# Reordering VectorE's period, one bank for the gate projection and the tail's last product in a convolution, state-space and expert kernel

## The chip, the cores and the metric

One core of one Trainium2 chip. The metric is the device time of one execution in microseconds; lower is better. The kernel before took 418.74 us, the median of 3 runs (417.58 to 419.7).

## The reference, cut to what matters

Three layers run over x of shape (16, 64, 16, 16) in float32: a graph convolution with group norm, a selective state-space layer on 64 features of 256 tokens for each of the 16 images, and a top-2-of-8 expert layer. The change touches the last two.

```python
# state-space layer, per token t (INNER = 128 channels, 16 states)
x_main, x_gate = split(ln(x) @ W_in + b_in)
xc = silu(x_main @ W_conv + b_conv)
B, C = split(xc @ W_bc + b_bc);  dt = softplus(xc @ W_dt + b_dt)
h = exp(dt * A) * h + dt * B * xc        # the scan over tokens
y = sum over states of (h * C)
t = t + (y * silu(x_gate)) @ W_out + b_out
# expert layer
xn = ln(ln(t));  logits = ln(t) @ Wr + br;  top 2 of 8, softmax weights
t = t + sum over the 2 chosen experts of w * (gelu(xe @ W1 + b1) @ W2 + b2)
```

## The kernel before, in words

The 16 images go in G = 8 groups of two; a group has T = 512 token columns on 128 partitions. The 2,048 state rows of a group (128 channels by 16 states) are 16 blocks of 128 rows, taken two at a time in 8 **slots**. A slot on VectorE is a product that forms the scan's input (L736, in the first group's slots 0 and 1 L731) and the scan itself (L743). GpSimd then multiplies the scan's result by C (`pool_slot`, L341), and TensorE sums over the states (`pe_sum`, L1023). The decay factors exp(dt * A) come from ScalarE (`act_decay`, L572), blocks 0 to 7 from a copy that DMA spreads over the partitions, blocks 8 to 15 from TensorE (`pe_spread`, L1098).

The loop over i has 8 **periods**, here called period 0 to period 7. In period i the slots of group i run; beside them goes the rest of group i - 1 (`prev`: gate product, output projection, norm, router, experts) and the beginning of group i + 2 (`nxt2`: first norm, projections). Nothing is planned by a program: each engine has its own hand-written order in its own `body`, and semaphores tie them together.

On VectorE a period is slot 0, `dve_relu` (L758, the softplus' linear part for group i + 1), `dve_gate` (L764, y times the silu of the gate), `dve_t1` (L768, projection plus residual, which waits for TensorE's `pe_po`, L1077), slot 1, then `dve_lnF` (L774), `dve_xn2` (L781 twice and L785 twice, the operand X2 of the first expert matrix, its high part), `dve_router1` (L790, L793, L796), `dve_xn` of group i + 2 (L749), `dve_router2` (ten small instructions, L803 to L822), slots 2 to 7 with the eight `dve_expert` (L830) from slot 4 on. `dve_router2` needs an exponential from ScalarE (`act_router`, L592), which ScalarE gives after `act_lnA2` (L517, L519) of group i + 2. GpSimd makes the low part of X2 by a subtraction (`pool_x2`, L366), and ends the router's weights (`pool_router`, L372 to L383). ScalarE's second half of a period is the experts' gelu (L610), then `act_siluz` (L526) and `act_silug` (L531) of group i + 2.

PSUM has 8 banks of 512 columns: 0 and 1 hold the scan's input, 2 B, then XD, XA, XB, XC = 3 to 6, and YS = 7. `pe_projg` (L1052) writes the gate projection into XC, which the experts' sums use too, and so waits for `me`, VectorE's reading of experts 4 and 5. `pe_warm` (L1174) issues matmuls whose result nobody reads.

After the last period the rest of group 7 runs with nothing beside it; this is called the **tail** here: gate, output projection, norm, router and experts. In period 7 the last product by C is GpSimd's like all others.

Of the kernel before, what the change touches and what calls it, by code (L numbers as in the profile page):

```python
# [70 lines left out]
def build(nc, x, cW1, cb1, Wl, bl, Wr, Wf, bf, cW2, cb2, W_in, b_in, W_conv, b_conv, A_log, W_bc, b_bc,  # L71
# [10 lines left out]
    with ctx:  # L82
# [140 lines left out]
        gp = nc.gpsimd  # L223

# [161 lines left out]
        def _(eng):  # L386
# [71 lines left out]
            def body(i, p, nxt, nxt2, prev):  # L458
# [36 lines left out]
                pool_slot(eng, i, p, 7)  # L495
# [7 lines left out]
            pool_x2(eng, G - 1)  # L503
# [24 lines left out]
        def act_silug(eng, g):  # L528
            eng.wait_ge(S["g_mm"], g + 1)
            since(eng, "yg", g - 2)  # L530
            a_.activation(sg[:, g % 3, :], P[:, XC, :], ACT.Silu, bias=cols[:, R["b_in"] + 1:R["b_in"] + 2]).then_inc(S["sg"], 1)  # L531
# [46 lines left out]

        def act_lnF2(eng, g):
            eng.wait_ge(S["var2"], g + 1)  # L580
            since(eng, "tn", g)
            a_.activation(rs2[:, :], P[:, XB, HW:T], ACT.Ln, bias=epst[:, 0:1]).then_inc(S["ln2"], 1)
            since(eng, "xn2", 2 * g)
            a_.activation(rqs[:, :], P[:, XB, HW:T], ACT.Ln, scale=1.0 + EPS, bias=eps2t[:, 0:1]).then_inc(S["lnq"], 1)
            eng.wait_ge(S["ln2"], g + 1)
            a_.activation(rs2[:, :], rs2[:, :], ACT.Exp, scale=-0.5).then_inc(S["rs2"], 1)
            eng.wait_ge(S["lnq"], g + 1)
            a_.activation(rqs[:, :], rqs[:, :], ACT.Exp, scale=-0.5).then_inc(S["rq"], 1)
# [24 lines left out]
        def _(eng):  # L613
# [22 lines left out]
            def body(i, p, nxt, nxt2, prev):  # L636

                q = 1 - p
                act_decay(eng, i, 4, 5, 6, 7)
# [13 lines left out]
                act_decay(eng, i, 12, 13)  # L653
                if nxt2 is not None:
                    act_lnA2(eng, nxt2)
                if prev is not None:
                    act_router(eng, prev)
# [45 lines left out]
            a_.preload_act_table_set("natural_log_exp_and_others")  # L703
            act_abs(eng, 1)
# [71 lines left out]
        def dve_xn2(eng, g):  # L776
            eng.wait_ge(S["rq"], g + 1)
            since(eng, "xl2", g)
            for h in range(2):
                q = slice(64 * h, 64 * h + 64)  # L780
                v.tensor_tensor(xnt2[:, HW * h:HW * h + HW], P[q, XB, 0:HW], rqs[q, :], ALU.mult).then_inc(S["xn2"], 1)  # L781
            since(eng, "f1", EXP * KC * g)
# [52 lines left out]
        def _(eng):  # L835
# [122 lines left out]
            def body(i, p, nxt, nxt2, prev):  # L958
# [11 lines left out]
                elif nxt is not None:  # L970
                    dve_relu(eng, nxt)
                if prev is not None:
                    dve_gate(eng, prev)
                    dve_t1(eng, prev, q)
                dve_slot(eng, i, 1)
                if i == 0:
                    dve_relu(eng, 1)
                if prev is not None:
                    dve_lnF(eng, prev)
                    dve_xn2(eng, prev)  # L980
                    dve_router1(eng, prev)
                if i > 0 and nxt2 is not None:
                    dve_xn(eng, nxt2)
                if prev is not None:
                    dve_router2(eng, prev)
                dve_slot(eng, i, 2)
                if i == 0:
# [418 lines left out]
```

## Time and profile before

| | us |
|---|---|
| median of 3 runs | 418.74 |
| the profiled execution | 418.46 |
| its span, first to last instruction | 416.7 |
| VectorE busy | 335.4 (80% of the span) |
| TensorE busy (ends are modelled) | 339.8 (82%) |
| ScalarE busy | 279.7 (67%) |
| GpSimd busy | 269.7 (65%) |

The profiled execution is 0.28 us below the median of the runs, and its span 1.8 us below its own time. Times of the trace count from the start of the span. A group of the page or a line of the timeline names the source line, engine, instruction, what it writes and reads, and in brackets how long the engine sat idle before it and what ended that wait.

### The profile page before, as it was taken

The numbers are of one execution on the slowest core, as the hardware profiler recorded it, in microseconds if no ns is written. First come the engines' busy times: TensorE is split into PE (matmuls) and PEld (weight loads), VectorE is DVE, ScalarE is ACT, GpSimd is POOL, SyncE is SP. The second block draws the span as 40 slices with busy tenths as digits, with TensorE's granted clock in tenths as the row PEclk, the third lists the DMA queues.
The fourth block names the chain that finished last, engine by engine and source line by source line (L and its number), as shares of the span: only waits on it lengthen the run. The fifth ranks groups of instructions, "written<-read, shape, count | busy, mean of one in ns | idle before, by whom it ended". The sixth has DMA issues, their size and how long they took to land. (4 is left out here: it accounts for less than half of the span.)

```text
span 416.7 us, 5478 instructions
## 1 busy us (share of the span) xinstructions
PE 339.8 (82%) x1651; PEld 181.9 (44%) x1651; DVE 335.4 (80%) x460; ACT 279.7 (67%) x458; POOL 269.7 (65%) x272
## 2 busy tenths in 40 slices
PE   0596896728898889888988999799789977996795
PEld 0483444412454345434543553455245524543452
DVE  2786456697899989998999899899989999992411
ACT  1002667736976996799779879987896767650563
POOL 9615125575559947995799489848975894683222
PEclk9996998668999999999999899999988998996999
DMA  8680089899769478769865887579767960000000
GB/s 198 194 155 4 0 208 226 218 230 226 186 160 212 115 192 194 170 138 196 206 165 132 201 201 170 142 170 223 167 150 167 223 145 0 2 0 14 1 0 13
DMA packets 21236, 59.52 MB, mean 143 GB/s; under 512 B 4924, under 2 KB 13272, under 8 KB 15320
## 3 DMA queue, kind: packets, MB, share of 16 engines
q1 hardware_dynamic: 20040, 58.34, 61.1%
q10 hardware_dynamic: 1168, 0.84, 0.8%
q8 instruction: 13, 0.21, 0.2%
q14 instruction: 15, 0.12, 0.1%
HBM read 53.93 MB, written 5.24 MB: 142 GB/s over the span
## 5 line engine op out<-in xcount | busy, mean ns | idle before, releaser
L341 POOL TENSOR_TENSOR hs<-hs,Cs 128x1024 f32<-128x1024 f32 x64 | 151.8, 2372 | 53.7 <-DVE hs L743 53.1
L743 DVE TENSOR_TENSOR_SCAN hs<-av,P 128x1024 f32<-128x1024 f32 x64 | 146.3, 2286 | 4.9 <-PE P L1023 2.0
L610 ACT ACTIVATE hb<-P,b1c 128x512 f32<-128x512 f32 x128 | 81.4, 683 | 21.5 <-PE P L1145 19.2
L736 DVE SCALAR_TENSOR_TENSOR P<-P,bbcol,ub 128x1024 f32<-128x1024 f32 x62 | 79.7, 1285 | 1.3
L1158 PE MATMUL P<-hb,W2s 128*64 128x256 f32 x512 | 68.7, 391 | 0.0
L1144 PE MATMUL P<-X,W1H 128*128 128x512 f32 x128 | 59.6, 465 | 5.2 <-ACT hb L610 3.3
L1145 PE MATMUL P<-X,W1L 128*128 128x512 f32 x128 | 52.2, 408 | 0.0
L353 POOL TENSOR_TENSOR accs<-accs,mes 128x256 f32<-128x256 f32 x56 | 40.9, 731 | 12.0 <-DVE mes L830 7.4
L572 ACT ACTIVATE av<-P,Aneg 128x510 f32<-128x510 f32 x68 | 44.0, 687 | 6.7 <-PE P L1098 5.4
L1158 PEld LDWEIGHTS P<-hb,W2s 128*64 128x64 f32 x512 | 31.3, 136 | 30.6 <-issue 20.5
L830 DVE SCALAR_TENSOR_TENSOR mes<-P,cols,wbs 128x256 f32<-128x256 f32 x64 | 27.3, 467 | 16.0 <-PE P L1158 9.6
L572 ACT ACTIVATE av<-av,Aneg 128x510 f32<-128x510 f32 x60 | 38.1, 707 | 0.1
L1144 PEld LDWEIGHTS P<-X,W1H 128*128 128x128 f32 x128 | 25.1, 196 | 26.9 <-ACT hb L610 15.9
L1098 PE MATMUL P<-D,selD 128*128 128x512 f32 x64 | 32.6, 535 | 4.9 <-ACT av L572 4.0
L1023 PE MATMUL P<-hs,selS 128*32 128x512 f32 x256 | 31.8, 623 | 5.3 <-POOL hs L341 5.3
L603 ACT ACTIVATE wbs<-P 128x512 f32<-128x512 f32 x32 | 19.1, 598 | 20.8 <-PE P L1132 20.8
L1145 PEld LDWEIGHTS P<-X,W1L 128*128 128x128 f32 x128 | 25.3, 198 | 2.8
L1174 PE MATMUL P<-W1H 128*128 128x512 f32 x62 | 21.9, 475 | 4.6 <-POOL X L366 4.6
L1098 PEld LDWEIGHTS P<-D,selD 128*128 128x128 f32 x64 | 11.8, 194 | 18.9 <-issue 18.3
L1023 PEld LDWEIGHTS P<-hs,selS 128*32 128x32 f32 x256 | 6.9, 112 | 28.6 <-issue 16.9
L366 POOL TENSOR_TENSOR X<-xnt,X 64x512 fp32r<-64x512 f32 x8 | 10.1, 1264 | 12.4 <-DVE X L785 10.9
L1062 PE MATMUL P<-xc,Wrep 128*128 128x512 f32 x16 | 9.8, 696 | 9.1 <-DVE P L736 9.1
(188 smaller groups left out, 489.7 us busy)
## 6 DMA issues: line engine op xcount, KB each, us to landing
ub<-u_scratch SPq DMA_DIRECT2D x31, 1024.0 KB, 10.7
av<-dt_scratch SPq DMA_DIRECT2D x15, 1024.0 KB, 7.2
dt_scratch<-dts SPq DMA_DIRECT2D x7, 256.0 KB, 2.8
u_scratch<-rl SPq DMA_DIRECT2D x7, 256.0 KB, 2.8
av<-in_L_conv_Wr SPq DMA_DIRECT2D x2, 576.0 KB, 7.2
av<-in_L_conv_Wl SPq DMA_DIRECT2D x2, 576.0 KB, 7.7
res<-in_x SPq DMA_DIRECT2D x4, 256.0 KB, 4.8
hb<-in_L_ffn_W SPq DMA_DIRECT2D x2, 512.0 KB, 6.1
```

Source lines behind the costliest of these rows:

```text
L341: gp.tensor_tensor(hs[:, at, :, :], hs[:, at, :, :], rep(Cs[:, p, :], 1, 2), ALU.mult).then_inc(S["cm"], 1)
L353: gp.tensor_tensor(acc[:, p, :], prev, mes[:, e % 4, :], ALU.add).then_inc(S["acc"], 1)
L572: a_.activation(steps, dt_of, ACT.Exp, scale=Aneg[:, m:m + 1]).then_inc(S["aexp"], 1)
L610: a_.activation(hb[:, r % 4, :], P[:, (XA, XB)[r % 2], :], ACT.Gelu, bias=b1c[:, r:r + 1]).then_inc(S["gl"], 1)
L736: v.scalar_tensor_tensor(out=ring, in0=rep(P[:, BB, :], 1, 2), scalar=bbcol[:, 0:1], in1=ub[:, 2 * n:2 * n + 2, :], op0=ALU.add, op1=ALU.m ...
L743: v.tensor_tensor_scan(hs[:, (SLOTS * g + n) % RING].rearrange("p a t -> p (a t)"), av[:, 2 * n:2 * n + 2, :].rearrange("p a t -> p (a t)" ...
L830: v.scalar_tensor_tensor(out=mes[:, e % 4, :], in0=P[:, (XC, XD)[e // 2 % 2], HW * (e % 2):HW * (e % 2) + HW], scalar=cols[:, R["b2"] + e: ...
L1023: last = pe.matmul(P[32 * q:32 * q + 32, YS, :], selS[:, k, :], hs[:, (SLOTS * g + n) % RING, q % 2, :], start=(k == 0), stop=(k == 3))
L1098: pe.matmul(P[:, (YS, XA)[m % 2], :], selD[:, m - BY_PE[0], :], D2[:, :], start=True, stop=True).then_inc(S["dt_pe"], 1)
L1144: pe.matmul(P[:, bank, :], W1H[:, e, 128 * k:128 * k + 128], X2[:, :], start=True, stop=False)
L1145: pe.matmul(P[:, bank, :], W1L[:, e, 128 * k:128 * k + 128], X2[:, :], start=False, stop=True).then_inc(S["f1"], 1)
L1158: last = pe.matmul(P[64 * h:64 * h + 64, (XC, XD)[pair % 2], HW * (e % 2):HW * (e % 2) + HW], W2s[:, e, k, :], hb[:, r % 4, HW * h:HW * h ...
```

## The change

In words: the gate projection of groups 2 to 7 goes to bank XB and waits for the previous gelus instead of `me`. VectorE runs the gate product ahead of the relu, and both router parts ahead of `dve_xn`; ScalarE gives the router's exponential ahead of `act_lnA2`. In the first period two decays (blocks 4 and 5) go ahead of ScalarE's softplus of group 1, the relu of group 1 behind slot 2, and the norm product of group 2 from behind slot 3 to behind slot 5. In a normal period 2 instead of 4 warming matmuls stand before the experts. In the last period VectorE does the last product by C itself, and 10 warming matmuls stand before the last sum over states. In the tail ScalarE makes the experts' scale before the router's, VectorE does the experts' operand around the router's and its low part, and 3 instead of 8 warming matmuls follow the router.

```diff
+        def gbank(g):
+            return XC if g < 2 else XB
...
   # GpSimd
                 weighted(4)
-                pool_slot(eng, i, p, 7)
+                if nxt is not None:
+                    pool_slot(eng, i, p, 7)
...
-            pool_x2(eng, G - 1)
             pool_router(eng, G - 1)
...
   # ScalarE: act_silug reads P[:, gbank(g), :] instead of P[:, XC, :]
...
         def act_lnF2(eng, g):
             eng.wait_ge(S["var2"], g + 1)
             since(eng, "tn", g)
             since(eng, "xn2", 2 * g)
+            since(eng, "xh2", 2 * g)
+            if g < G - 1:
+                act_rs2(eng, g)
+                act_rq(eng, g)
+                act_rs2_exp(eng, g)
+                act_rq_exp(eng, g)
+            else:
+                act_rq(eng, g)
+                act_rs2(eng, g)
+                act_rq_exp(eng, g)
+                act_rs2_exp(eng, g)
...
-                act_decay(eng, i, 4, 5, 6, 7)
+                act_decay(eng, i, *((4, 5, 6, 7) if i > 0 else (6, 7)))
...
                 act_decay(eng, i, 12, 13)
+                if prev is not None:
+                    act_router(eng, prev)
                 if nxt2 is not None:
                     act_lnA2(eng, nxt2)
-                if prev is not None:
-                    act_router(eng, prev)
...
             a_.preload_act_table_set("natural_log_exp_and_others")
+            act_decay(eng, 0, 4, 5)
             act_abs(eng, 1)
             act_softplus(eng, 1)
...
   # VectorE: dve_xn2 gets an argument, called between its two xnt2 products and its two X2 products
...
                 dve_slot(eng, i, 0)
                 if i == 0:
                     dve_xn(eng, 1)
-                elif nxt is not None:
+                if prev is not None:
+                    dve_gate(eng, prev)
+                if i > 0 and nxt is not None:
                     dve_relu(eng, nxt)
                 if prev is not None:
-                    dve_gate(eng, prev)
                     dve_t1(eng, prev, q)
                 dve_slot(eng, i, 1)
-                if i == 0:
-                    dve_relu(eng, 1)
                 if prev is not None:
                     dve_lnF(eng, prev)
                     dve_xn2(eng, prev)
                     dve_router1(eng, prev)
+                    dve_router2(eng, prev)
                 if i > 0 and nxt2 is not None:
                     dve_xn(eng, nxt2)
-                if prev is not None:
-                    dve_router2(eng, prev)
                 dve_slot(eng, i, 2)
+                if i == 0:
+                    dve_relu(eng, 1)
...
                 dve_slot(eng, i, 3)
-                if i == 0:
-                    dve_xn(eng, 2)
                 dve_slot(eng, i, 4)
                 experts(0)
                 dve_slot(eng, i, 5)
+                if i == 0:
+                    dve_xn(eng, 2)
                 experts(2)
...
                 dve_slot(eng, i, 7)
+                if nxt is None:
+                    last = hs[:, (SLOTS * G - 1) % RING, :, :]
+                    eng.wait_ge(S["cm"], SLOTS * G - 1)
+                    eng.wait_ge(S["scan"], SLOTS * G)
+                    v.tensor_tensor(last, last, rep(Cs[:, p, :], 1, 2), ALU.mult).then_inc(S["cm"], 1)
                 experts(6)
...
             dve_t1(eng, G - 1, 1)
-            dve_lnF(eng, G - 1)
+            dve_xn2(eng, G - 1, lambda: dve_lnF(eng, G - 1))
+            eng.wait_ge(S["xh2"], 2 * G)
+            v.tensor_tensor(X2[64:128, :], xnt2[:, :], X2[0:64, :], ALU.subtract).then_inc(S["xl2"], 1)
             dve_router1(eng, G - 1)
-            dve_xn2(eng, G - 1)
             dve_router2(eng, G - 1)
...
   # TensorE
         def pe_projg(eng, g):
-            since(eng, "cs", g)
-            if g == 1:
-                eng.wait_ge(S["sg"], 1)
-            since(eng, "me", EXP * (g - 2) - 2)
+            if g < 2:
+                since(eng, "cs", g)
+                since(eng, "sg", g)
+            since(eng, "gl", EXP * KC * (g - 2))
...
-                    pe_warm(eng, 4, XB)
+                    pe_warm(eng, 2, XB)
...
                 for k in range(4):
+                    if k == 3 and nxt is None:
+                        pe_warm(eng, 10, XB)
                     pe_sum(eng, i, k)
...
             pe_router(eng, G - 1)
-            pe_warm(eng, 8)
+            pe_warm(eng, 3)
```

## Rows read from the trace of the kernel before

**Rows 1.** Windows view: most of period 3; two microseconds of period 4.
```profile
core 0: us, PE busy (x) PEld busy (x) DVE busy (x) ACT busy (x) POOL busy (x), PEclk, DMA share, GB/s
181.00:221.00 40.00, 35.60 (x182) 18.21 (x182) 37.53 (x48) 33.70 (x57) 30.97 (x28) 1.00 0.78 176
232.00:234.00 2.00, 2.00 (x6) 1.15 (x4) 1.93 (x6) 1.36 (x2) 1.07 (x5) 0.50 1.09 233
```

**Rows 2.** Timeline of VectorE, period 4: start us, us, instruction, idle before.
```profile
222.56 0.48 DVE L768 SCALAR_TENSOR_TENSOR t1s<-P,cols,res 128x256 f32<-128x256 f32 x1 [0.76 <-PE P L1077]
...
230.18 0.42 DVE L749 TENSOR_TENSOR xnt<-P,rs 128x256 f32<-128x256 f32 x1 [0.90 <-ACT rs L519]
...
232.40 1.28 DVE L736 SCALAR_TENSOR_TENSOR P<-P,bbcol,ub 128x1024 f32<-128x1024 f32 x1
```

**Rows 3.** Timeline of VectorE, period 7, which has no relu and no first norm.
```profile
340.50 0.69 DVE L764 TENSOR_TENSOR ygs<-P,sg 128x512 f32<-128x512 f32 x1 [0.18 <-PE P L1023]
341.95 0.48 DVE L768 SCALAR_TENSOR_TENSOR t1s<-P,cols,res 128x256 f32<-128x256 f32 x1 [0.76 <-PE P L1077]
...
348.96 0.97 DVE L803 SCALAR_TENSOR_TENSOR rt<-rt,rank 128x32 f32<-128x32 f32 x1 [0.30 <-ACT rt L592]
...
351.64 1.28 DVE L736 SCALAR_TENSOR_TENSOR P<-P,bbcol,ub 128x1024 f32<-128x1024 f32 x1
```

**Rows 4.** Timeline of GpSimd, its subtraction for X2 in periods 4 and 7.
```profile
229.23 1.26 POOL L366 TENSOR_TENSOR X<-xnt,X 64x512 fp32r<-64x512 f32 x1 [0.23 <-POOL hs L341]
...
348.62 1.26 POOL L366 TENSOR_TENSOR X<-xnt,X 64x512 fp32r<-64x512 f32 x1 [0.23 <-POOL hs L341]
```

**Rows 5.** Timeline of TensorE, the gate projection in period 3.
```profile
212.90 1.10 PE L1052 MATMUL P<-xnt,Wgs 128*128 128x256 f32 x4 [1.24 <-DVE mes L830]
```

**Rows 6.** Timeline of VectorE, period 0 and the first scan of period 1.
```profile
61.45 1.23 DVE L731 TENSOR_TENSOR P<-P,hs 128x1024 f32<-128x1024 f32 x1 [1.76 <-PE P L1109]
...
67.59 0.75 DVE L758 TENSOR_SCALAR rl<-P,cols 128x512 f32<-128x512 f32 x1 [2.58 <-ACT sp L536]
...
70.28 2.29 DVE L743 TENSOR_TENSOR_SCAN hs<-av,P 128x1024 f32<-128x1024 f32 x1 [0.74 <-DVE P L736]
...
79.82 0.42 DVE L749 TENSOR_TENSOR xnt<-P,rs 128x256 f32<-128x256 f32 x1 [3.60 <-ACT rs L519]
...
91.16 1.29 DVE L736 SCALAR_TENSOR_TENSOR P<-P,bbcol,ub 128x1024 f32<-128x1024 f32 x1
...
98.17 2.29 DVE L743 TENSOR_TENSOR_SCAN hs<-av,P 128x1024 f32<-128x1024 f32 x1 [1.97 <-PE P L1023]
```

**Rows 7.** Timeline of ScalarE, period 0: softplus of group 1, decays 8 and 9.
```profile
66.87 0.69 ACT L536 ACTIVATE sp<-P,cols 128x512 f32<-128x512 f32 x1
...
72.34 1.26 ACT L572 ACTIVATE av<-P,Aneg 128x510 f32<-128x510 f32 x2 [0.92 <-POOL rl L328]
```

**Rows 8.** Page, DMA issues: KB each, median us from issue to landing.
```profile
ub<-u_scratch SPq DMA_DIRECT2D x31, 1024.0 KB, 10.7
```

**Rows 9.** Timeline of VectorE, the last scan and the tail.
```profile
373.19 2.29 DVE L743 TENSOR_TENSOR_SCAN hs<-av,P 128x1024 f32<-128x1024 f32 x1
...
379.95 0.69 DVE L764 TENSOR_TENSOR ygs<-P,sg 128x512 f32<-128x512 f32 x1 [3.71 <-PE P L1023]
...
387.84 0.20 DVE L790 TENSOR_TENSOR P<-P,brs 128x32 f32<-128x32 f32 x1 [0.71 <-PE P L1115]
...
390.66 0.96 DVE L807 TENSOR_TENSOR rt<-rt,rv 128x32 f32<-128x32 f32 x1
```

**Rows 10.** Timeline of GpSimd, its subtraction for X2 in the tail.
```profile
390.31 1.26 POOL L366 TENSOR_TENSOR X<-xnt,X 64x512 fp32r<-64x512 f32 x1 [10.86 <-DVE X L785]
```

**Rows 11.** Timeline of TensorE, the last sum over states.
```profile
377.95 1.94 PE L1023 MATMUL P<-hs,selS 128*32 128x512 f32 x8 [3.58 <-POOL hs L341]
```

**Rows 12.** Timeline of ScalarE, first logarithm of the second norm, period 7 and tail.
```profile
344.70 0.47 ACT L582 ACTIVATE rs2s<-P,epst 128x256 f32<-128x256 f32 x1 [0.21 <-PE P L1087]
...
385.53 0.47 ACT L582 ACTIVATE rs2s<-P,epst 128x256 f32<-128x256 f32 x1 [1.28 <-PE P L1087]
```

More of the change, by code:

```diff
@@ L530, in act_silug @@
             since(eng, "yg", g - 2)
-            a_.activation(sg[:, g % 3, :], P[:, XC, :], ACT.Silu, bias=cols[:, R["b_in"] + 1:R["b_in"] + 2]).then_inc(S["sg"], 1)
+            a_.activation(sg[:, g % 3, :], P[:, gbank(g), :], ACT.Silu, bias=cols[:, R["b_in"] + 1:R["b_in"] + 2]).then_inc(S["sg"], 1)
         def act_abs(eng, g):
@@ L577, in act_lnF1, with act_rs2, act_rq, act_rs2_exp @@
             a_.activation(sq2[:, :], P[:, XB, 0:HW], ACT.Square).then_inc(S["sq2"], 1)
+        def act_rs2(eng, g):
+            a_.activation(rs2[:, :], P[:, XB, HW:T], ACT.Ln, bias=epst[:, 0:1]).then_inc(S["ln2"], 1)
+        def act_rq(eng, g):
+            a_.activation(rqs[:, :], P[:, XB, HW:T], ACT.Ln, scale=1.0 + EPS, bias=eps2t[:, 0:1]).then_inc(S["lnq"], 1)
+        def act_rs2_exp(eng, g):
+            eng.wait_ge(S["ln2"], g + 1)
+            a_.activation(rs2[:, :], rs2[:, :], ACT.Exp, scale=-0.5).then_inc(S["rs2"], 1)
+        def act_rq_exp(eng, g):
+            eng.wait_ge(S["lnq"], g + 1)
+            a_.activation(rqs[:, :], rqs[:, :], ACT.Exp, scale=-0.5).then_inc(S["rq"], 1)
         def act_lnF2(eng, g):
@@ L581, in act_lnF2 @@
             since(eng, "tn", g)
-            a_.activation(rs2[:, :], P[:, XB, HW:T], ACT.Ln, bias=epst[:, 0:1]).then_inc(S["ln2"], 1)
             since(eng, "xn2", 2 * g)
[L584 to L588, printed above, removed]
+            since(eng, "xh2", 2 * g)
[9 more added lines that the diff above has]
+                act_rs2_exp(eng, g)
         def act_router(eng, g):
@@ L774, in dve_lnF, with dve_xn2 @@
             v.tensor_tensor(tns[:, :], P[:, XB, 0:HW], rs2[:, :], ALU.mult).then_inc(S["tn"], 1)
-        def dve_xn2(eng, g):
+        def dve_xn2(eng, g, between=None):
             eng.wait_ge(S["rq"], g + 1)
@@ L781, in dve_xn2 @@
                 v.tensor_tensor(xnt2[:, HW * h:HW * h + HW], P[q, XB, 0:HW], rqs[q, :], ALU.mult).then_inc(S["xn2"], 1)
+            if between is not None:
+                between()
             since(eng, "f1", EXP * KC * g)
@@ L1046, in pe_projg @@
         def pe_projg(eng, g):
-            since(eng, "cs", g)
-            if g == 1:
-                eng.wait_ge(S["sg"], 1)
-            since(eng, "me", EXP * (g - 2) - 2)
+            if g < 2:
+                since(eng, "cs", g)
+                since(eng, "sg", g)
+            since(eng, "gl", EXP * KC * (g - 2))
             for h in range(2):
-                last = pe.matmul(P[:, XC, HW * h:HW * h + HW], Wgs[:, h, :], xnt[:, :], start=True, stop=True)
+                last = pe.matmul(P[:, gbank(g), HW * h:HW * h + HW], Wgs[:, h, :], xnt[:, :], start=True, stop=True)
             last.then_inc(S["g_mm"], 1)
```

## The prediction

> **What bounds the kernel now.** I read the windows first, then the timeline of VectorE, then the waits that interrupt it, and only then the other engines. Over 40 us that are most of period 3, VectorE is busy 37.53 of 40.00 us, TensorE 35.60 at full clock, ScalarE 33.70 and GpSimd 30.97 [rows 1]. VectorE runs its slots back to back and has two stops in a normal period: 0.76 us ahead of t1, while TensorE forms the output projection, and 0.90 us ahead of the first norm's product, while ScalarE ends its scale [rows 2]. So VectorE sets the length of the six periods 1 to 6, and an edit there is worth what it takes from these stops. At both ends of the kernel VectorE is not full: in period 0 it stands 2.58, 0.74 and 3.60 us [rows 6], and in the tail one engine waits for another all along. There each link of the chain counts.
>
> **Gate ahead of relu (periods 1 to 6).** Period 7 has no relu and shows the new order: the gate product starts after 0.18 us of waiting for the sum over states, and t1 follows 1.45 us after the gate (341.95 - 340.50) [rows 3]. The relu (0.75 [rows 6]) now fits between them, since 0.69 + 0.75 = 1.44. The stop of 0.76 goes, 0.18 comes: 0.58 at most. Some of it is lost because an instruction that waits can't start under the end of the one before (an estimate, 0.08 at each of the two places). I take 0.4, with 0.2 and 0.58 as bounds: 6 x 0.4 = 2.4 us. The relu's reader on GpSimd is still busy with an older product by C then, and is not made late.
>
> **Router ahead of the first norm (periods 1 to 5).** Meant to remove the 0.90. But period 7 again shows the new order: 0.30 us of waiting for ScalarE's exponential, and then an L803 of 0.97 us, where it computes only 32 columns [rows 3]; L790, as small, takes 0.20 [rows 9]. Its end, 348.96 + 0.97 = 349.93, lies at the end of GpSimd's subtraction for X2, 348.62 + 1.26 = 349.88 [rows 4]. In the tail L803 comes ahead of that subtraction, and it is L807 that takes 0.96 and ends at 391.62, with the subtraction ending at 391.57 [rows 9, 10]. Both instructions read two tensors from SBUF, as the subtraction does. So I read 0.78 us as a hold by GpSimd. In period 4 the subtraction ends at 230.49, just ahead of where L803 comes behind the norm product, which starts at 230.18 [rows 2, 4]: the wait of 0.90 hid the hold. From the end of L796 to slot 2 it takes 0.90 + (232.40 - 230.18) = 3.12 us now; in the new order 0.30 + (351.64 - 348.96) = 2.98 [rows 2, 3], plus 0.42 for the norm product, whose scale is long there: 3.40. That is a loss of 0.28 a period, 5 x 0.28 = 1.4 us. Without the hold it would be 3.40 - 0.78 = 2.62, a gain of 0.5 a period. I take the hold, because two such lengths end together with the same neighbour.
>
> The Trainium skill (SBUF - State Buffer, section "Who interferes with whom") says that a VectorE instruction with two SBUF inputs and a GpSimd instruction that reads SBUF exclude each other, the later one waiting for the whole of the first. By it every one of periods 1 to 5 pays the hold (408.7 in all); were the long instructions something else, the sum would be 404.8.
>
> **Gate projection in XB.** TensorE's wait of 1.24 for `me` goes [rows 5], and ScalarE's silu and table load come that much earlier. VectorE has no wait on ScalarE's decays in a period, so this is off the path: 0, with VectorE's slot 7 as the cover. The two warming matmuls less also cost or give nothing there, as ScalarE's gelu table is the later one. All of it gives slack, and if the cover went it would be worth at most 1.2 a period.
>
> **Period 0.** Slot 1's scan ends at 67.59 - 2.58 = 65.0. Now: the relu waits, slot 2's scan starts at 70.28 because decay 5 is late, slot 4 waits 3.60 for the norm, and slot 7's input product ends at 91.16 + 1.29 = 92.45 [rows 6]. After: decays 4 and 5 take ScalarE's place at 66.87 and end at 66.87 + 1.26 = 68.13 (the price of two from decays 8 and 9) [rows 7]. Slot 2's input product needs only its load (a chunk lands 10.7 us after its issue [rows 8], in the median) and is done by then. Scan 68.2 to 70.5; relu to 71.25. GpSimd's step for group 1, which started when softplus was ready 2.2 us earlier, starts there, and decays 8 and 9, which wait for it at 72.34, start at 74.5 and end at 75.8 [rows 7]. VectorE meanwhile: input product, scan, input product (0.15 + 1.29 + 2.29 + 1.29) to 76.3, so it barely waits. Scan to 78.6, product to 79.9, scan to 82.2. The norm's scale, ready at 79.8, comes at 82.0, no wait. Norm 0.4, then product, scan, product: 87.4. That is 92.45 - 87.4 = 5.0 us. The first scan of period 1 comes 98.17 - 92.45 = 5.72 us after that point, behind TensorE's work that starts there [rows 6], and moves with it. What could be late next: the load of u's first chunk for group 1, behind a write that is issued 2.2 us later (needed by 90 to 92, expected at 89), and GpSimd's restart behind slot 7's product, which I work out at 92.3 against a scan at 93.1. Bounds 2.0 (one of them late) and 5.9 (TensorE at full clock in that stretch).
>
> **Tail.** (a) The last scan ends at 373.19 + 2.29 = 375.48; GpSimd's last product is behind its accumulations, and the sum starts at 377.95 and takes 1.94 at half clock after TensorE sat idle 3.58 [rows 9, 11]. VectorE's product costs 1.23 (the nearest row is L731 of the same shape, with one input in PSUM [rows 6]), so the sum can start at 376.8; ten warming matmuls keep TensorE busy until then, and at full clock it takes half, 1.0. The gate, now at 379.95, comes at 377.9: 2.0 us. The experts' instructions behind the product (0.85) end before. (b) From the gate to the norm's first logarithm it is 385.53 - 379.95 = 5.58 in the tail, and 344.70 - 340.50 = 4.20 in period 7 [rows 3, 9, 12]; the difference is TensorE's half clock. I take 1.3; bounds 0 and 1.4. (c) After it: the wait of 0.71 for the router's product goes under the experts' operand, the hold of 0.96 - 0.20 = 0.76 goes with GpSimd's subtraction [rows 9]; VectorE's subtraction adds 0.62 (half of 1.23) ahead of the router, and the exponential is waited for, 0.30 [rows 3]. 0.71 + 0.76 - 0.62 - 0.30 = 0.55, taken as 0.5; bounds -0.3 and 1.2. After that TensorE runs on as before. The tail gives 3.8.
>
> **Sum.** 2.4 - 1.4 + 5.0 + 2.0 + 1.3 + 0.5 = 9.8 us. The profiled execution took 418.46, so 408.7; it lies 0.28 below the median, which is less than I can resolve, and I predict 408.7.
>
> **Rivals.** No hold in the router: all as above, but the router gains 0.5 a period instead of losing 0.28, 3.9 us more, 404.8. Against it are two coincidences of ends within 0.1 us; for it, that five of these periods showed no long instruction. Period 0 is worth only 2.0 because a load or GpSimd's restart is late: 411.7. For it, everything there is chained; against, each has some slack. The tail's clock does not hold, so the change doesn't do what it says there: the sum costs 1.94 again and (b) gives nothing, 2.2 less, 410.9. Slower: with two warming matmuls instead of four TensorE's clock stays at half through the experts. It fell there even with four, to 0.50 at 232 to 234 [rows 1]. TensorE has 4.40 us idle in a period, and a us at half clock adds 0.5 of work, so from 9 us of half clock a period on it would become the bound. At 13 us in each of 7 periods it costs 6.5 - 4.4 = 2.1 each, 14.7, and gives 418.46 - 9.8 + 14.7 = 423.4. Against it, the row at 0.50 has TensorE fully busy, which is what brought the clock back each time.
>
> **Numbers.** The forecast has 0.62, no hold 0.08, a short period 0 0.17, the tail's clock 0.08, the clock in the periods 0.03; 0.02 is left for a change within the noise. The range 405.0 to 412.0 holds the first, third and fourth with their bounds. About 0.5%, 2.1 us, is what a measurement of this kernel can tell from no change; faster means under 416.6. Faster 0.95, same 0.02, slower 0.03.
>
> **What would show it.** In a normal period: gate first with a wait near 0.2, no wait ahead of t1, an L803 near 0.97 in periods 1 to 7 and no wait ahead of the norm product; a period of 39.8 us instead of 40. Slot 7's input product of period 0 ending at 87.4. The gate of the tail 2.5 us after the last scan instead of 4.5, its sum at about 1.0 us, and no long router instruction. An L803 of 0.18 in periods 1 to 5, a new wait ahead of slots 4 to 6 of period 0 or of slot 0 of period 1, or a TensorE clock of 0.5 over most of the experts would make the prediction wrong.

## The result, and the profile after

The changed kernel takes 408.27 us in the median of 4 runs (406.66 to 409.93), beside 419.06 us (417.58 to 419.7, 4 runs) for the kernel before (its 418.74 further up came from the first three of these runs): a ratio of 0.9751, with a 95% interval of 0.9715 to 0.9787. The forecast was 408.7, in a range of 405.0 to 412.0. The profiled execution of the changed kernel is the slowest of its four, 409.93 us with a span of 408.2; before, the span was 416.7. So the spans differ by 8.5 us, where the forecast's sum was 9.8, and the first question is which terms make 8.5.

I cut both spans at the same points: the start of slot 0's scan in each period, and the start of the last scan. From VectorE's timelines these are 57.09, 98.17, 138.34, 178.32, 218.28, 258.24, 298.22, 338.03 and 373.19 before, and 56.70, 92.61, 132.23, 171.99, 211.73, 251.50, 291.26, 330.69 and 367.17 after.

| stretch | before | after | gained | forecast |
|---|---|---|---|---|
| to the first scan | 57.09 | 56.70 | 0.39 | 0 |
| period 0 | 41.08 | 35.91 | 5.17 | 5.0 |
| periods 1 to 6 | 239.86 | 238.08 | 1.78 | 1.0 |
| period 7 to its last scan | 35.16 | 36.48 | -1.32 | 0 |
| last scan to the end | 43.51 | 41.03 | 2.48 | 3.8 |
| span | 416.7 | 408.2 | 8.5 | 9.8 |

Two lines are off by more than 1 us, period 7 and the tail. First the middle, VectorE's timeline after, in period 2 (start us, us, instruction, idle before it):

```profile
134.68 0.69 DVE L788 TENSOR_TENSOR ygs<-P,sg 128x512 f32<-128x512 f32 x1 [0.17 <-PE P L1055]
135.28 0.74 DVE L782 TENSOR_SCALAR rl<-P,cols 128x512 f32<-128x512 f32 x1
136.12 0.48 DVE L792 SCALAR_TENSOR_TENSOR t1s<-P,cols,res 128x256 f32<-128x256 f32 x1
...
142.64 0.19 DVE L822 TENSOR_TENSOR rt<-P,rv 128x32 f32<-128x32 f32 x1
143.13 0.98 DVE L829 SCALAR_TENSOR_TENSOR rt<-rt,rank 128x32 f32<-128x32 f32 x1 [0.30 <-ACT rt L615]
...
145.82 0.42 DVE L773 TENSOR_TENSOR xnt<-P,rs 128x256 f32<-128x256 f32 x1
146.15 1.28 DVE L760 SCALAR_TENSOR_TENSOR P<-P,bbcol,ub 128x1024 f32<-128x1024 f32 x1
```

The wait of 0.76 ahead of t1 [rows 2] is gone and 0.17 ahead of the gate has come. The wait of 0.90 ahead of the norm product [rows 2] is gone too, and a router instruction of 32 columns, L829 (L803 before), takes 0.98. From the step between the scans of slots 0 and 1 the period gains 0.38 to 0.42 (0.66 in period 1), from the router's step it loses 0.18 or 0.19 in periods 2 to 5 and 0.10 in period 1. In period 1 L829 takes 0.90, in periods 2 to 6 0.97 to 0.99. The group of L829 over the whole kernel (count, shortest/median/longest in ns, first and last start):

```profile
L829 DVE SCALAR_TENSOR_TENSOR rt<-rt,rank x8: 192/973/987, 103.5 to 381.0; 128x32 f32<-128x32 f32 x8
its engine sat idle before it (us, times) until:
  ACT rt L615: 2.4, 8
```

And who was beside it in period 2, GpSimd's timeline after:

```profile
142.80 1.27 POOL L370 TENSOR_TENSOR X<-xnt,X 64x512 fp32r<-64x512 f32 x1 [0.23 <-POOL hs L345]
```

This subtraction ends at 142.80 + 1.27 = 144.07 and L829 at 143.13 + 0.98 = 144.11. In the tail, where no subtraction of GpSimd stands beside it any more, L829 takes 0.19.

Period 0 came close to what was worked out. VectorE's timeline after, there:

```profile
65.77 1.29 DVE L760 SCALAR_TENSOR_TENSOR P<-P,bbcol,ub 128x1024 f32<-128x1024 f32 x1 [1.15 <-DMA ub<-u_scratch]
67.90 2.29 DVE L767 TENSOR_TENSOR_SCAN hs<-av,P 128x1024 f32<-128x1024 f32 x1 [0.83 <-ACT av L576]
70.10 0.73 DVE L782 TENSOR_SCALAR rl<-P,cols 128x512 f32<-128x512 f32 x1
...
82.30 0.43 DVE L773 TENSOR_TENSOR xnt<-P,rs 128x256 f32<-128x256 f32 x1
82.64 1.28 DVE L760 SCALAR_TENSOR_TENSOR P<-P,bbcol,ub 128x1024 f32<-128x1024 f32 x1
...
86.28 1.29 DVE L760 SCALAR_TENSOR_TENSOR P<-P,bbcol,ub 128x1024 f32<-128x1024 f32 x1
87.61 2.29 DVE L767 TENSOR_TENSOR_SCAN hs<-av,P 128x1024 f32<-128x1024 f32 x1
90.03 1.29 DVE L760 SCALAR_TENSOR_TENSOR P<-P,bbcol,ub 128x1024 f32<-128x1024 f32 x1
92.61 2.29 DVE L767 TENSOR_TENSOR_SCAN hs<-av,P 128x1024 f32<-128x1024 f32 x1 [1.29 <-PE P L1055]
```

Of the waits of 2.58, 0.74 and 3.60 us [rows 6] the first and the last are gone. The new wait of 1.15 for a load of u costs nothing, because slot 2's scan still waits 0.83 for its decay behind it. Slot 7's input product ends at 86.28 + 1.29 = 87.57 (forecast 87.4).

Period 7 lost 1.32 us, for another reason. The windows after (us; busy us and count of PE, PEld, DVE, ACT, POOL; granted TensorE clock; DMA share; GB/s), first where period 7 lost its time, then two stretches of the tail:

```profile
333.00:335.00 2.00, 1.19 (x9) 0.37 (x5) 0.69 (x1) 0.00 (x0) 2.00 (x2) 0.56 0.80 167
335.00:337.00 2.00, 2.00 (x5) 1.49 (x6) 1.92 (x3) 1.24 (x2) 0.81 (x1) 0.50 0.19 42
337.00:339.00 2.00, 2.00 (x7) 1.53 (x6) 2.00 (x1) 1.10 (x3) 0.00 (x0) 0.50 0.00 0
384.00:385.20 1.20, 0.86 (x4) 0.13 (x2) 0.00 (x0) 1.10 (x2) 0.51 (x3) 0.68 0.00 0
385.20:387.20 2.00, 2.00 (x10) 0.82 (x9) 0.00 (x0) 0.37 (x1) 0.00 (x0) 0.50 0.04 8
```

From 333 to 339 the granted clock is 0.56 and then 0.50, TensorE's lower level of 1.2 GHz. VectorE then waits 1.23 us for the output projection ahead of t1 (0.76 before [rows 3]) and 1.30 ahead of L798, the second norm's product, where it had no wait before. Of the profiled executions of the changed kernel and of its eleven variants below, this one and that of the last product back on GpSimd show this fall. The kernel under "Warming in the tail" has the same instructions as the changed one up to its tail and nearly the same idle times of TensorE here (1.71 and 0.81 us; in the changed kernel 1.67 and 0.81), but its profile shows a clock of 1.00 from 333 to 341 and takes 35.18 us where this one takes 36.48. So the fall is not a property of the edit: some executions have it and some don't. One profile of each kernel can't say how many.

The tail, in TensorE's timeline after:

```profile
370.84 1.06 PE L1055 MATMUL P<-hs,selS 128*32 128x512 f32 x8 [0.62 <-DVE hs L1030]
...
383.06 0.51 PE L1176 MATMUL P<-X,W1H 128*128 128x512 f32 x1 [1.75 <-ACT hb L633]
...
384.71 0.61 PE L1155 MATMUL P<-ident,vv 128*32 128x128 f32 x2 [0.34 <-POOL vv L387]
385.25 1.98 PE L1190 MATMUL P<-hb,W2s 128*64 128x256 f32 x8
```

The sum takes 1.06 in place of 1.94 [rows 11]. The gate starts at 371.98, 2.52 us after the last scan's end (369.46), where it was 379.95 - 375.48 = 4.47 [rows 9]. The norm's first logarithm comes at 376.05, 4.07 behind the gate instead of 5.58 [rows 12]. The router's transposes come 8.66 us after that, instead of 9.13. Up to here the tail has gained 1.95 + 1.51 + 0.47 = 3.93 us. Then it loses: from the transposes to VectorE's last experts' instructions (403.06) it takes 18.35 us, and it took 16.93 (411.59 - 394.66). The row of 1.98 us is the first of the experts' second products; the same eight took 1.08 before. TensorE had stood 1.75 us for a gelu and 0.34 for the router, and the windows above show its clock falling to 0.68 and then 0.50. This fall, too, is not in every execution, as "Warming in the tail" shows.

### The profile page after: what moved, and what is told of

It reads as the page before. It is cut to its first block and busy times, and to the rows that moved or that the text cites. A ratio compares the mean times of both kernels' runs of the same rounds, so it can differ in the third digit from the quotient of the medians.

```text
span 408.2 us, 5461 instructions
## 1 busy us (share of the span) xinstructions
PE 338.1 (83%) x1642; PEld 181.1 (44%) x1642; DVE 337.5 (83%) x462; ACT 281.3 (69%) x458; POOL 265.9 (65%) x270
## 5 line engine op out<-in xcount | busy, mean ns | idle before, releaser
L345 POOL TENSOR_TENSOR hs<-hs,Cs 128x1024 f32<-128x1024 f32 x63 | 149.2, 2372 | 44.9 <-DVE hs L767 44.3
L1190 PE MATMUL P<-hb,W2s 128*64 128x256 f32 x512 | 70.0, 397 | 0.0
L1130 PE MATMUL P<-D,selD 128*128 128x512 f32 x64 | 34.6, 565 | 7.1 <-ACT av L576 4.7
L1055 PE MATMUL P<-hs,selS 128*32 128x512 f32 x256 | 30.8, 598 | 6.4 <-POOL hs L345 5.8
L1130 PEld LDWEIGHTS P<-D,selD 128*128 128x128 f32 x64 | 12.7, 206 | 21.6 <-issue 20.8
L1206 PE MATMUL P<-W1H 128*128 128x512 f32 x53 | 18.5, 456 | 4.4 <-POOL X L370 4.4
L376 POOL TENSOR_TENSOR rt<-rt,rv 128x32 f32<-128x32 f32 x8 | 1.9, 239 | 24.2 <-DVE rt L848 24.2
L1164 PE MATMUL P<-wT,selW 32*128 32x256 f32 x64 | 16.1, 330 | 0.0
```

Of the source, the lines that this page charges most:

```text
L345: gp.tensor_tensor(hs[:, at, :, :], hs[:, at, :, :], rep(Cs[:, p, :], 1, 2), ALU.mult).then_inc(S["cm"], 1)
L1055: last = pe.matmul(P[32 * q:32 * q + 32, YS, :], selS[:, k, :], hs[:, (SLOTS * g + n) % RING, q % 2, :], start=(k == 0), stop=(k == 3))
L1130: pe.matmul(P[:, (YS, XA)[m % 2], :], selD[:, m - BY_PE[0], :], D2[:, :], start=True, stop=True).then_inc(S["dt_pe"], 1)
L1190: last = pe.matmul(P[64 * h:64 * h + 64, (XC, XD)[pair % 2], HW * (e % 2):HW * (e % 2) + HW], W2s[:, e, k, :], hb[:, r % 4, HW * h:HW * h ...
```

## The experiments

Two theories stood at the start. The first is the forecast's: GpSimd's subtraction holds L829, and the terms are those of the table. Its rival: the lengths of about 0.97 come from something else (the place in the order, the wait ahead), and the gain lies elsewhere. Later a second question came: what TensorE's clock did. The medians of the kernel before, taken again beside the experiments, lie between 417.69 and 419.06 us, so effects under 1.5 us are read from the profiles, period by period.

### Router parts in the old order

VectorE's second router part goes behind the norm product again, and ScalarE's exponential behind `act_lnA2`. The part on VectorE:

```diff
-                    dve_router2(eng, prev)
                 if i > 0 and nxt2 is not None:
                     dve_xn(eng, nxt2)
+                if prev is not None:
+                    dve_router2(eng, prev)
```

> The changed kernel with the router's order of the kernel before (norm product between the two router parts, ScalarE's exponential behind the first norm). Theory (the long first router instruction is a hold by GpSimd's subtraction): that instruction is 0.18 us in periods 1 to 5 and stays near 0.97 in periods 6 and 7, a wait of 0.9 is back ahead of the norm product, and each of periods 1 to 5 is 0.19 us shorter than in the changed kernel, about 1 us in all. Rival (the order is a gain, the length comes with any wait for ScalarE): the periods are 0.5 us longer each, 2.5 us in all.

Measured: 408.06 us (405.88 to 408.79, 6 runs), ratio 0.9753 [0.9721, 0.9785], span 405.5. VectorE's timeline in period 3 of this kernel:

```profile
182.56 0.43 DVE L773 TENSOR_TENSOR xnt<-P,rs 128x256 f32<-128x256 f32 x1 [0.91 <-ACT rs L523]
182.90 0.18 DVE L829 SCALAR_TENSOR_TENSOR rt<-rt,rank 128x32 f32<-128x32 f32 x1
```

The hold goes and the wait comes back in periods 1 to 5. In periods 6 and 7, whose order this edit leaves alone, the instruction still takes 0.98. Periods 2 to 5 are 39.58 to 39.62 us long, 0.12 to 0.18 shorter than in the changed kernel, so this part of the change is a loss of about that much in each of them, as the direction of the forecast had it. Over the kernel that is under 1 us, and the medians (0.2 apart) can't show it. The span is 2.7 us shorter mostly because this execution had no fall in period 7 (1.33) and reached its first scan 1.39 us earlier; it gave 1.07 back in period 1, where the granted clock fell to 0.50 (96 to 98 us) and VectorE waited 0.95 ahead of L798.

### A second subtraction on GpSimd

```diff
             gp.tensor_tensor(X2[64:128, :], xnt2[:, :], X2[0:64, :], ALU.subtract)
+            gp.tensor_tensor(X2[64:128, :], xnt2[:, :], X2[0:64, :], ALU.subtract)
```

The second is ordered behind the first and writes the same numbers again.

> The changed kernel with GpSimd's subtraction for X2 done twice, one behind the other (the same numbers again). Theory (GpSimd holds VectorE's instructions with two SBUF inputs for the whole of its own instruction, and each instruction is held by itself): the first router instruction stays near 0.97, and the next one with two SBUF inputs, the third of the ten, becomes long too and ends with the second subtraction, some 1.2 us longer per period in 1 to 7, 8 us in all. Rival (no hold): no router instruction changes its length, and VectorE's periods stay as they are, since the experts have slack; no change of time.

Measured: 414.3 us (414.07 to 414.86, 4 runs), ratio 0.9909 [0.9878, 0.994], span 412.3. VectorE's timeline in period 2 of this kernel, and then GpSimd's:

```profile
144.62 0.88 DVE L831 SCALAR_TENSOR_TENSOR rt<-rt,rank 128x32 f32<-128x32 f32 x1 [0.29 <-ACT rt L617]
145.53 0.18 DVE L833 TENSOR_REDUCE rv<-rt 128x4 f32<-128x32 f32 x1
145.75 1.09 DVE L835 TENSOR_TENSOR rt<-rt,rv 128x32 f32<-128x32 f32 x1
146.87 0.19 DVE L837 SCALAR_TENSOR_TENSOR rt<-rt 128x32 f32<-128x32 f32 x1
```

```profile
144.18 1.27 POOL L370 TENSOR_TENSOR X<-xnt,X 64x512 fp32r<-64x512 f32 x1 [0.23 <-POOL hs L345]
145.52 1.26 POOL L372 TENSOR_TENSOR X<-xnt,X 64x512 fp32r<-64x512 f32 x1
```

The first subtraction ends at 145.45 and L831 at 145.50. The second, issued at 145.52, takes a second instruction with it: L835, with two inputs in SBUF, ends at 146.84, beside 146.78. The reduction between them, with one input, keeps its 0.18. From slot 1's scan to slot 2's each of periods 1 to 6 is 0.88 to 0.91 us longer, which is 1.09 - 0.19 = 0.90. So the hold is GpSimd's, it lasts to the end of GpSimd's instruction, and the neighbour with one input doesn't pay. I had expected 1.2 us a period; the second hold is one instruction's length less what VectorE does before it meets the next such instruction.

The Trainium skill (SBUF - State Buffer, section "Who interferes with whom") has the two exclude each other for a whole instruction. The traces agree in the one direction that they show, VectorE waiting for GpSimd: 0.98 and 1.09 us in place of 0.19.

### Slot 2's input product between the router's parts

If the hold is per instruction, an instruction without two SBUF inputs put beside the subtraction hides it. The input product of slot 2 reads PSUM and one SBUF tensor, takes 1.28 us, and also covers the wait for ScalarE's exponential. `dve_input` and `dve_scan` are the two halves of `dve_slot`.

```diff
                     dve_router1(eng, prev)
+                dve_input(eng, i, 2)
+                if prev is not None:
                     dve_router2(eng, prev)
                 if i > 0 and nxt2 is not None:
                     dve_xn(eng, nxt2)
-                dve_slot(eng, i, 2)
+                dve_scan(eng, i, 2)
```

> The changed kernel with slot 2's input product (1.28 us, one input in SBUF) put between the two router parts on VectorE, its scan left behind them. Theory (hold): the product covers both the 0.30 of waiting for ScalarE and the hold of 0.78, so the first router instruction is 0.2 us in every period, and periods 1 to 7 are each 1.0 to 1.1 us shorter, some 7 us in all, to about 401. Rival (the first router instruction is long in itself behind this work): it stays near 0.97, and only the wait of 0.30 goes, 2 us in all.

Measured: 401.49 us (399.4 to 402.46, 6 runs), ratio 0.9596 [0.9567, 0.9625], span 400.2. Its VectorE timeline in period 3:

```profile
180.59 0.19 DVE L831 TENSOR_TENSOR rt<-P,rv 128x32 f32<-128x32 f32 x1
180.70 1.28 DVE L765 SCALAR_TENSOR_TENSOR P<-P,bbcol,ub 128x1024 f32<-128x1024 f32 x1
181.89 0.18 DVE L838 SCALAR_TENSOR_TENSOR rt<-rt,rank 128x32 f32<-128x32 f32 x1
```

and GpSimd's, at the same time:

```profile
180.71 1.27 POOL L370 TENSOR_TENSOR X<-xnt,X 64x512 fp32r<-64x512 f32 x1 [0.23 <-POOL hs L345]
```

Both run for their usual time side by side. Periods 2 to 6 come to 38.22 to 38.84 us (39.43 to 39.77 in the changed kernel), 0.92 to 1.26 less in the router's step, about the hold of 0.80 and the wait of 0.30 together. Period 1 gains only 0.22 us. In all, the expectation of some 7 us is met (408.27 to 401.49). So the rival of the forecast, in which the router's new order gains 0.5 a period, was wrong for the change but can be had, and more, by one line's move.

### Warming in the tail

```diff
             pe_pair(eng, G - 1, 0)
+            pe_warm(eng, 7)
             pe_f1(eng, G - 1, 2)
```

> The changed kernel with 7 more warming matmuls in the tail, between the first expert pair's first matrix and the second's, where TensorE sat idle 1.75 us. Theory (the 1.4 us that the chain behind the router's transposes is longer than before is TensorE's clock, which fell to half there): the clock stays at 1.00 there, the stretch from the transposes to the last expert product is 16.9 us instead of 18.35, and the time is 1.4 us less. Rival (the clock falls by itself, whatever stands there): the same 18.35, or longer by what the warming matmuls delay, up to 0.3.

Measured: 407.69 us (406.77 to 407.96, 5 runs), ratio 0.9743 [0.9715, 0.9771], span 406.1. TensorE's timeline of this kernel:

```profile
380.64 1.55 PE L1206 MATMUL P<-W1H 128*128 128x512 f32 x6
...
383.98 0.39 PE L1155 MATMUL P<-ident,vv 128*32 128x128 f32 x2 [0.35 <-POOL vv L387]
384.31 1.08 PE L1190 MATMUL P<-hb,W2s 128*64 128x256 f32 x8
```

The stretch from the transposes to the last experts' instructions is 400.91 - 383.98 = 16.93 us, to the hundredth what it was before the change, and the granted clock stays at 1.00 through it. So the 1.42 us lost in the tail are the clock's: the same eight matmuls take 1.08 us at 1.00 and 1.98 where it fell. What made it fall is not shown. The doubled subtraction's kernel has the changed kernel's 3 warming matmuls, none of the 7, and the same idle times, and its clock holds as well (TensorE's timeline):

```profile
388.58 0.50 PE L1178 MATMUL P<-X,W1H 128*128 128x512 f32 x1 [1.75 <-ACT hb L635]
...
390.24 0.39 PE L1157 MATMUL P<-ident,vv 128*32 128x128 f32 x2 [0.35 <-POOL vv L389]
390.56 1.08 PE L1192 MATMUL P<-hb,W2s 128*64 128x256 f32 x8
```

The stretch takes 16.93 us in the profiles of four kernels without the 7 matmuls (doubled subtraction, last product on GpSimd, gate projection at its old place with either order), and 17.86 to 18.49 in five (the changed one, router in the old order, slot 2's product first, period 0 in the old order, relu first). All three kernels with the 7 have 16.93. That fits the theory, but three executions without a fall can also be chance where four of nine have none. The medians differ by 0.6, which their scatter does not resolve.

### Period 0 in the old order

```diff
-                act_decay(eng, i, *((4, 5, 6, 7) if i > 0 else (6, 7)))
+                act_decay(eng, i, 4, 5, 6, 7)
...
-            act_decay(eng, 0, 4, 5)
```

On VectorE the relu goes back behind slot 1 and the norm product behind slot 3.

> The changed kernel with period 0 as before (decays 4 and 5 behind the softplus of group 1, relu behind slot 1, norm product behind slot 3). Theory: the first scan of period 1 comes 41.1 us after the first of period 0 instead of 35.9, with waits of 2.6 and 3.6 back on VectorE, and the time is 5.2 us longer, about 413.2. Rival (the loads bound period 0 and its start only moved the wait): under 2 us longer.

Measured: 414.46 us (412.23 to 415.16, 4 runs), ratio 0.9891 [0.985, 0.9932], span 412.7. Period 0 takes 41.33 us beside 35.91, and VectorE's timeline has its two waits back:

```profile
67.77 0.75 DVE L781 TENSOR_SCALAR rl<-P,cols 128x512 f32<-128x512 f32 x1 [2.58 <-ACT sp L540]
...
80.09 0.42 DVE L772 TENSOR_TENSOR xnt<-P,rs 128x256 f32<-128x256 f32 x1 [3.69 <-ACT rs L523]
```

So about half of the change's gain is in its first period, 5.42 us here and 5.17 in the table.

### The last product back on GpSimd

```diff
-                if nxt is not None:
-                    pool_slot(eng, i, p, 7)
+                pool_slot(eng, i, p, 7)
```

VectorE's product and its waits go.

> The changed kernel with the last product by C on GpSimd again, the ten warming matmuls left in. Theory (the product's place and GpSimd's queue set the gate's start): the gate comes 3.6 us after the last scan's end instead of 2.5 (GpSimd's product ends at 2.4 as before, the sum takes 1.05 at full clock since the warming matmuls keep TensorE busy), 1.1 us longer in all. Rival (VectorE's product gave nothing, the warming did it): the gate comes at 2.5 as in the changed kernel.

Measured: 409.01 us (408.46 to 411.35, 4 runs), ratio 0.9783 [0.9748, 0.9818], span 409.6. Timeline of all engines of this kernel, in the tail:

```profile
369.89 2.35 POOL L345 TENSOR_TENSOR hs<-hs,Cs 128x1024 f32<-128x1024 f32 x1 [0.33 <-DVE hs L766]
...
372.30 1.06 PE L1049 MATMUL P<-hs,selS 128*32 128x512 f32 x8 [1.72 <-POOL hs L345]
373.43 0.69 DVE L787 TENSOR_TENSOR ygs<-P,sg 128x512 f32<-128x512 f32 x1 [2.84 <-PE P L1049]
```

The gate comes 373.43 - 369.82 = 3.61 us after the last scan's end, 1.1 later than in the changed kernel (2.52) and 0.9 earlier than before (4.47). So of the 1.95 us of term (a), 1.1 is the product's 1.23 in place of 2.35, and the sum at full clock (1.06 in place of 1.94) is the other 0.9. The ten warming matmuls stand ahead of the sum in both kernels; none was run without them, so that they made the clock is argued and not shown. Behind the gate this execution differs once more: the clock falls to 0.50 from 375 to 377, and the norm's first logarithm comes 5.46 us after the gate and not 4.07. Its experts' stretch has no fall, so the two nearly cancel, and that the tail is the expected 1.1 us longer in all is partly luck. The medians are 0.7 apart, which they can't resolve.

### Relu ahead of the gate again

```diff
-                if prev is not None:
-                    dve_gate(eng, prev)
                 if i > 0 and nxt is not None:
                     dve_relu(eng, nxt)
+                if prev is not None:
+                    dve_gate(eng, prev)
```

> The changed kernel with the relu ahead of the gate product again. Theory: the stop of 0.76 ahead of t1 is back in periods 1 to 6, the wait of 0.17 ahead of the gate goes, each of these periods is 0.4 us longer, 2.4 us in all. Rival (GpSimd's queue sets slot 1 anyway): the stop is back and the periods keep their length.

Measured: 412.22 us (411.13 to 412.86, 4 runs), ratio 0.9846 [0.9819, 0.9873], span 411.1. That is 3.9 us more than the changed kernel's median, and 2.4 were expected. The periods are 0.4 longer (period 1 0.66), as expected, and periods 3 to 5 another 0.5. TensorE's timeline of this kernel, in period 3, and its windows there:

```profile
172.58 1.04 PE L1055 MATMUL P<-hs,selS 128*32 128x512 f32 x8
174.44 1.06 PE L1055 MATMUL P<-hs,selS 128*32 128x512 f32 x8 [0.82 <-POOL hs L345]
176.71 1.12 PE L1109 MATMUL P<-ygs,Wouts 128*64 128x256 f32 x4 [1.20 <-DVE ygs L788]
```

```profile
176.00:178.00 2.00, 1.29 (x5) 0.54 (x6) 0.77 (x3) 0.72 (x2) 2.00 (x1) 0.65 0.57 125
178.00:180.00 2.00, 2.00 (x5) 1.45 (x6) 1.97 (x3) 1.39 (x3) 1.92 (x3) 0.50 0.04 10
```

TensorE waits 0.82 us for the last product by C and then 1.20 for the gate, and its clock falls; the output projection takes 1.12 in place of 0.65, and the chain behind it is late. In periods 2 and 6 of the same execution the two waits are as long (0.83 and 1.19), and the clock stays at 1.00. The first wait is there because the gate projection, which used to stand just ahead of the sums, has gone elsewhere. The next two kernels test that.

### Gate projection at its old place, with and without the relu first

The gate projection goes back to bank XC, waiting for `me`; the first kernel also has 4 warming matmuls again.

```diff
-            return XC if g < 2 else XB
+            return XC
...
-            since(eng, "gl", EXP * KC * (g - 2))
+            since(eng, "me", EXP * (g - 2) - 2)
```

> The changed kernel with the gate projection in XC again, waiting for experts 4 and 5, and with 4 warming matmuls ahead of the experts. Theory (both are off the path): the periods keep their length of 39.7 to 39.8, TensorE's wait of 1.24 for the gate projection is back, and its idle time between the sums over states (0.8) is gone; 408.3, within 0.7. Rival (VectorE or GpSimd feels the later silu): the periods are 0.3 us or more longer each.

Measured, with the gate ahead of the relu: 407.1 us (406.95 to 410.25, 4 runs), ratio 0.9754 [0.9697, 0.9811], span 405.2, periods 1 to 5 of 39.63 to 39.80 us and period 6 of 39.44, those of the changed kernel. TensorE's timeline of it in period 3:

```profile
170.03 3.87 PE L1055 MATMUL P<-hs,selS 128*32 128x512 f32 x32
174.72 0.65 PE L1109 MATMUL P<-ygs,Wouts 128*64 128x256 f32 x4 [0.81 <-DVE ygs L788]
```

The 32 sums run in one piece, without the wait for the last product, and the period is not shorter: the forecast's 0 for this part holds.

> The changed kernel with the relu first, as in e7_relu_first, and the gate projection in XC again, waiting for experts 4 and 5. Theory (the periods 3 to 5 of e7_relu_first that were 0.9 us and not 0.4 longer had TensorE's clock at half, because the early gate projection moved TensorE's idle time next to its wait for the gate): the sums over states run without a gap again, the clock stays at 1.00 there, and periods 1 to 6 are each 0.4 us longer than in the changed kernel, 2.4 in all, to about 410.8. Rival (the relu's order alone lets the clock fall): periods of 40.6 as in e7_relu_first, about 412.2.

Measured, with the relu first: 409.89 us (409.43 to 411.85, 4 runs), ratio 0.9804 [0.9762, 0.9847], span 408.5. Periods 2 to 5 are 40.15 or 40.16 us, 0.4 longer than in the changed kernel, and the window at 178 to 180 shows a clock of 1.00 where the kernel above showed 0.50. With the wait of 0.82 gone, the 1.20 alone brought no fall at this place in periods 2 to 6, where both together brought one in three of five periods above, and the changed kernel, with 0.8 and 0.81, has none there either. That makes the pair of waits the likely cause of the extra 0.5 us, from one execution of each kernel. In period 1 this kernel does fall to 0.50 (98 to 100 us), and that period takes 41.02 us. So the expectation is met in periods 2 to 6 and missed in period 1.

### Put together

Slot 2's input product between the router's parts, the 7 warming matmuls in the tail, and 6 ahead of the last sum of period 6.

```diff
...
-                    if k == 3 and nxt is None:
-                        pe_warm(eng, 10, XB)
+                    if k == 3 and nxt2 is None:
+                        pe_warm(eng, 10 if nxt is None else 6, XB)
```

> Slot 2's input product between the router parts, the 7 warming matmuls between the tail's first expert pairs, and 6 warming matmuls ahead of the last sum of period 6. Theory: the parts add up. Periods as with the input product alone, no fall of TensorE's clock behind the tail's transposes (1.4 us) and none at the start of period 7 (1.3 us where it falls): 399.5 to 400.5 against 401.5. Rival (the parts compete, or the clock falls elsewhere): 401.5 or more.

Measured: 400.29 us (399.83 to 401.75, 4 runs), ratio 0.957 [0.9543, 0.9597] to the kernel before, span 398.3. The periods 1 to 6 are 38.21 to 39.18 us, the last scan starts at 358.31 and the stretch from the transposes is 16.93 again. It is 8.0 us below the changed kernel in the median and within what was expected. Beside the kernel with slot 2's product alone (401.49, 399.4 to 402.46) it is not resolved: its range lies within that one's. The 6 matmuls of period 6 show nothing of their own, since period 7 takes 33.95 us here and 33.92 there.

> e8_combined with the gate projection in XC again and 4 warming matmuls ahead of the experts. Theory (moving the gate projection gave nothing but TensorE idle time next to the gate): the same periods of 38.4 to 38.8, and 400.3 within 0.7. Rival (with the shorter periods ScalarE has less room and the early gate projection is needed): periods over 39, 402 or more. Second rival (the clock fell in some of e8_combined's periods because of it): periods of 38.4 throughout, 399.5.

The same with the gate projection at its old place and 4 warming matmuls: 402.5 us (401.32 to 403.06, 6 runs), ratio 0.9621 [0.9577, 0.9664], span 399.7. The expectations are not met: the time is that of the first rival, and the periods are not. Periods 1 to 6 take 232.4 us in place of 231.6, and period 0 took 0.4 less, so the last scan starts only 0.30 later (358.61). Most of the difference in span, 1.4 us, lies just behind it. VectorE's waits for the sum ahead of the gate add up to 3.0 us in place of 1.9, and nearly all of this is one wait, in the tail: 1.81 in place of 0.81. TensorE had worked without a pause and reached the 10 warming matmuls at 361.21 (359.89 in the other kernel), and the last sum behind them started at 363.70, although VectorE's product was done at 361.00 + 1.23 = 362.23. So in the shorter periods TensorE's backlog reaches the tail, and there the warming matmuls delay the sum that they were meant to speed up. Which of the two edits, the projection's place or the two more warming matmuls a period, makes TensorE late was not separated, and of the 2.2 us between the medians 0.8 stay open.

## Why the prediction was right

**Gate ahead of relu.** Right: 0.38 to 0.42 a period against 0.4, with 0.66 in period 1; 2.64 us in all for 2.4. Undoing it costs 0.4 a period where the clock holds.

**Router order.** Right in sign and mechanism, and the second subtraction shows the mechanism. The size was off: 0.18 or 0.19 a period and 0.84 in all, in place of 0.28 and 1.4. From the end of L822 (142.83) to slot 2 (146.15) it takes 3.32 us, not 3.40: the norm product was charged with its 0.42, but the next instruction starts 0.33 after it. The length of L829 was right, 0.97 to 0.99 (0.90 in period 1). Period 7 had L829 at 0.47 only, since GpSimd's subtraction had begun 0.85 us ahead of it there (0.33 in period 2) and ended at 343.85, beside 343.91 for L829.

**Gate projection.** Right, 0: its removal leaves the periods as they are. What I did not see is that it changes where TensorE is idle. With the relu first, three periods cost 0.5 more, and none of periods 2 to 6 did with the projection at its old place.

**Period 0.** 5.17 us for 5.0, with two things behind it that offset. Slot 2's scan began at 67.90 (forecast 68.2), and its input product was done by then, as forecast, in spite of the wait of 1.15 for its load. From there to the end of slot 7's input product VectorE lost 0.47 more than forecast, by two waits of 0.15 and 0.32 for decays. That end, 87.57, is only 0.17 late, because this execution had reached its first scan 0.39 earlier; counted from the first scan, the gain up to there is 4.5 us and not 5.0. And the first scan of period 1 came 5.04 us after that product, not 5.72, with TensorE at full clock from 89 on, where the kernel before had 0.50 until 97; the forecast had this as its upper bound.

**Tail.** (a) 1.95 for 2.0, (b) 1.51 for 1.3 and just beyond its bound of 1.4, (c) 0.47 for 0.5. The weak step is the sentence "After that TensorE runs on as before". The change takes 5 of 8 warming matmuls away there, and that was costed at nothing, without a term or a rival. In this execution the clock fell behind the wait of 1.75 us, and the stretch cost 1.42 us. In four of nine profiles with 3 warming matmuls and none of the 7, TensorE did run on as before, at 16.93 us. That the 5 matmuls fewer let it fall is likely and not shown: no kernel was run with 8 again, and the kernel before has one profile.

**Period 7.** Not foreseen, 1.32 us in this execution. Together with the tail's 1.42 it takes 2.74 of the 11.2 us gained elsewhere. The forecast's rival of a clock not held in the tail (410.9) put that loss at the sum and the norm, where the clock did hold; the fall came behind them.

So it is in part luck that the forecast's total (408.7 for a median of 408.27) is that near: the periods gave 0.8 more than it had, the start 0.4, period 0 another 0.2, and the tail and period 7 took 2.6 more than it had in the profiled execution, which is 1.7 us above the median. Without its two falls that execution would be at some 407.2 (an estimate, 409.93 - 2.74), and the forecast, which had none of either, at 408.7.

## What to carry to other kernels

When an instruction of 0.2 us takes 1, compare its end with the neighbour's: if they end together, put an instruction without two SBUF inputs there, rather than moving the short one. Where an edit takes warming or other work from TensorE, look at the granted clock in the instructions behind, and in more than one execution: the same code held it in one and lost 1.3 us in another. And look at the first period and the tail as closely as at the loop: here six middle periods gave 1.8 us, and one reordered start 5.2.

## What the runs showed of the hardware

The held instruction ends 0.04 to 0.06 us after GpSimd's (periods 2 and 7 of the changed kernel, both subtractions of the doubled one), wherever it began: it is 0.28 us longer in period 7 (0.47 instead of 0.19), about 0.80 and 0.90 in the rows of period 2. After it, the next instruction takes its usual length unless GpSimd starts another. A product of 1.28 us with one SBUF and one PSUM input, beside the same subtraction, is not lengthened at all, nor is the subtraction (1.27).

TensorE's granted clock fell to 0.50, the level of 1.2 GHz, amid work with short idle times: 1.67 and 0.81 us in period 7 of the changed kernel, 1.75 and 0.34 in its tail, 0.82 and 1.20 in periods 3 to 5 of the kernel with the relu first. But the same idle times also went without a fall: 1.71 and 0.81 in period 7 of the kernel with warming in the tail, 1.75 and 0.35 in the tail of the doubled subtraction, 0.83 and 1.19 in periods 2 and 6 of the kernel with the relu first. In the kernel before, TensorE stood 1.88, 0.31 and 0.22 us at the same place of the tail, behind 8 warming matmuls, and kept 1.00 through 390 to 400 us. So in these traces the lengths of the idle times alone don't tell whether the clock falls. Where it fell, the eight second products took 1.98 us in place of 1.08.
